# The norms of two graph layers: sums of squares and the last scaling on ScalarE, in pieces one row apart

## The reference

```python
h_self = x @ W1[i] + b1[i]
h_nb = x @ W0[i] + b0[i]
agg = segment_sum(h_nb[edge_src], edge_dst, num_segments=n)
x = concatenate([h_self, agg], axis=-1) @ W2[i] + b2[i]
x = x / std(x, axis=-1, ddof=1, keepdims=True)
```

## Time and profile before

| | us |
|---|---|
| median of 3 runs | 2557.65 |
| lowest, highest | 2557.43, 2562.71 |
| the profiled execution's own time | 2560.65 |
| its span | 2558.9 |

### The profile page before, as it was taken

One profiled execution on the slowest core, in us unless ns is written; L12 is line 12 of the kernel. 1 busy time (PEld: TensorE's weight loads), 2 busy tenths in 40 slices (PEclk: granted clock), 3 DMA queues, 4 the chain that ended last, 5 costly groups with the idle time before them and its releaser, 6 DMA issues. The chain is left out here.

```text
span 2558.9 us, 59508 instructions
## 1 busy us (share of the span) xinstructions
PE 2064.3 (81%) x23672; PEld 1900.6 (74%) x23672; DVE 1740.2 (68%) x4728; ACT 885.0 (35%) x1180; POOL 1249.9 (49%) x1021
## 2 busy tenths in 40 slices
PE   4494569999999999997883897888887578888870
PEld 4232269999999999997883896777776567777760
DVE  8999975555555555565655995776676456777656
ACT  0395510000000000001211563777674066777620
POOL 0200047777777777760000452666664346666651
PEclk9995579999999999998996898999999689999975
DMA  3593012232323232320003882334433034434321
GB/s 130 170 408 130 1 19 25 21 30 21 30 21 30 21 30 21 30 21 14 1 1 125 301 319 68 114 120 129 133 114 115 19 92 129 125 114 133 122 78 28
DMA packets 150635, 227.44 MB, mean 89 GB/s; under 512 B 87617, under 2 KB 109793, under 8 KB 147074
## 3 DMA queue, kind: packets, MB, share of 16 engines
q1 hardware_dynamic: 70418, 186.31, 20.1%
q0 software_dynamic: 74688, 28.51, 11.5%
q10 hardware_dynamic: 5296, 9.47, 1.2%
HBM read 123.37 MB, written 100.84 MB: 88 GB/s over the span
## 5 line engine op out<-in xcount | busy, mean ns | idle before, releaser
L637 PE MATMUL ps<-parts,at 128*128 128x192 f16 x11250 | 947.9, 248 | 23.6 <-POOL at L669 13.7
L637 PEld LDWEIGHTS ps<-parts,at 128*128 128x128 f16 x11250 | 940.1, 99 | 25.9 <-issue 24.2
L1706 PE MATMUL ps<-yparts,source_onehots_c 128*128 128x192 f16 x7000 | 679.3, 250 | 123.6 <-issue 110.4
L1706 PEld LDWEIGHTS ps<-yparts,source_onehots_c 128*128 128x128 f16 x7000 | 579.1, 99 | 188.7 <-issue 172.0
L679 POOL DMA_INDIRECT weight_matrix<-w,place x392 | 609.6, 1555 | 175.0 <-issue 93.8
L1498 POOL DMA_INDIRECT messages_c<-y_table,srci_sb x504 | 498.2, 988 | 380.2 <-PE ps L1706 157.4
L767 DVE SCALAR_TENSOR_TENSOR t<-ps,coef,g 128x96 f32<-128x96 f32 x400 | 127.1, 318 | 246.4 <-PE ps L637 200.6
L1581 DVE TENSOR_SCALAR source_onehots_c<-sources_spread,shift 128x1280 f16<-128x1280 f16 x512 | 282.1, 561 | 0.4
L707 ACT ACTIVATE ea_limbs<-ea_in,ea_scale 128x392 f16<-128x392 f32 x32 | 19.9, 622 | 743.6 <-DMA ea_in<-in_eaT 735.4
L1526 ACT ACTIVATE source_gaps_c<-sources_spread,unshift 128x1280 f16<-128x1280 f16 x188 | 256.4, 1364 | 23.3 <-DVE source_onehots_c L1581 5.1
L1630 DVE SCALAR_TENSOR_TENSOR messages_c<-messages_c,brk 128x96 f32<-128x96 f32 x784 | 249.6, 318 | 17.4 <-issue 0.2
(11 more groups left out here) (374 smaller groups left out, 1858.5 us busy)
## 6 DMA issues: line engine op xcount, KB each, us to landing
weight_matrix<-blank SPq DMA_DIRECT2D x27, 1600.0 KB
weights<-weight_matrix SPq DMA_DIRECT2D x25, 1728.0 KB
run_max<-messages_c SPq DMA_DIRECT2D x28, 960.0 KB
ea_c<-edge_limbs SPq DMA_DIRECT2D x28, 896.0 KB
edge_limbs<-ea_limbs SPq DMA_DIRECT2D x128, 98.0 KB
run_max<-messages_c SPq DMA_DIRECT2D x28, 384.0 KB
sources_spread<-sources_by_tile ACTq DMA_DIRECT2D x26, 320.0 KB
messages_c<-y_table,srci_sb POOLq DMA_INDIRECT x504
```

Source lines behind the costliest of these rows:

```text
L637: mm = nc.tensor.matmul(m.ps[:, bank, 0:2 * D], m.at[:, s, blk * P:(blk + 1) * P], parts[:, s, :], start=(s == 0), stop=(s == NB - 1))
L1706: return nc.tensor.matmul(m.ps[:, i // 2, at:at + 2 * D], hot[:, b, i * P:(i + 1) * P], parts[:, b, :], start=(b == 0 and i % 2 == 0), sto ...
```

## The change

For groups 0 to 3 of both layers (`beside`), the norm is cut into pieces that stand one row step apart. VectorE sums the rows and writes the negative mean (`negative_mean`). ScalarE then runs five ACTIVATEs with the function Square, one per block of 128x96, with the negative mean as a bias pointer and the sum over the row as accumulator output (`sum_squares`). One step on VectorE turns the sums into variances (`spread_of`) and ScalarE takes the root. One more step on VectorE refines the root and scales `y` (`unit_spread`); in the second layer the scaling and the residual are one instruction per block, with the root as a pointer, followed by the layer norm's negative mean. The layer norm goes the same way, two rows later: squares by ScalarE four rows behind, variance and root five behind, refinement and a shift (minus mean times inverse root) on VectorE six behind, and then ScalarE writes `x` by five ACTIVATEs with the function Identity, scale and bias as pointers. The last group of each layer keeps the old pieces at their old places. `norms` numbers the norms for the semaphores, `closing(i, lag)` names the group whose last row stands `lag` rows back. TensorE's program is unchanged.

```diff
@@ -861,7 +861,12 @@
         mx, amx, scales = sem("y_max"), sem("y_max_all"), sem("scale_known")
         highs, ready = sem("y_high_parts"), sem("y_parts")
         b = c.enter_context(nc.Block())
+        meaned, squared, shifts = sem("group_means"), sem("squares_summed"), sem("norm_shifts")
+        xs = sem("x_scaled")
         last_of = lambda q: q % ENDS == ENDS - 1
+        closing = lambda i, lag: (i - lag) // ENDS if 0 <= i - lag < NB and last_of(i - lag) else None
+        beside = lambda g: g is not None and g < NEND - 1
+        norms = lambda layer, g: (NEND - 1) * layer + (g if layer == 0 else 2 * g)
         ends = lambda g: slice(g * ENDS, (g + 1) * ENDS)
 
         @b.sync
@@ -883,6 +888,14 @@
 
         @b.scalar
         def _(a):
+            def sum_squares(n, g):
+
+                a.wait_ge(meaned, n + 1)
+                for j, q in enumerate(range(g * ENDS, (g + 1) * ENDS)):
+                    summed = nc.scalar.activation(deep[:, j, :], y[:, q, :], ACT.Square, bias=m.st1[:, q:q + 1],
+                                                  accum_out=m.st2[:, q:q + 1])
+                summed.then_inc(squared, 1)
+
             for layer in range(2):
                 back = 1.0 / XSCALE if layer == 0 else un[:]
                 roots = ROOTS_SAGE + layer * NEND
@@ -910,12 +923,30 @@
                             a.wait_ge(outd, n - 2)
                         nc.scalar.activation(aggT[:, (n - 1) % 2, :], m.ps[0:D, 4 + (n - 1) % 2, 0:P],
                                              ACT.Copy).then_inc(aggtc, 1)
-                    if 2 <= i <= NB + 1 and last_of(i - 2):
-                        g = (i - 2) // ENDS
+                    g = closing(i, 2)
+                    if beside(g):
+                        sum_squares(norms(layer, g), g)
+                    elif g is not None:
                         square_root(nc, a, m, roots + (g if layer == 0 else 2 * g) + 1, m.st2[:], ends(g))
-                    if layer == 1 and 3 <= i <= NB + 2 and last_of(i - 3):
-                        g = (i - 3) // ENDS
+                    g = closing(i, 3)
+                    if beside(g):
+                        square_root(nc, a, m, roots + (g if layer == 0 else 2 * g) + 1, m.st2[:], ends(g))
+                    elif g is not None and layer == 1:
                         square_root(nc, a, m, roots + 2 * g + 2, m.st2[:], ends(g))
+                    if layer == 1:
+                        g = closing(i, 4)
+                        if beside(g):
+                            sum_squares(norms(layer, g) + 1, g)
+                        g = closing(i, 5)
+                        if beside(g):
+                            square_root(nc, a, m, roots + 2 * g + 2, m.st2[:], ends(g))
+                        g = closing(i, 6)
+                        if beside(g):
+                            a.wait_ge(shifts, g + 1)
+                            for q in range(g * ENDS, (g + 1) * ENDS):
+                                moved = nc.scalar.activation(m.x[:, q, :], y[:, q, :], ACT.Identity, bias=m.st1[:, q:q + 1],
+                                                             scale=m.st2[:, q:q + 1])
+                            moved.then_inc(xs, 1)
                 if layer == 0:
                     a.wait_ge(scales, 1)
                     for g in range(NEND):
@@ -953,6 +984,33 @@
                 do(nc.vector.tensor_reduce(m.st2[:, blk], deep[:], AX.X, ALU.add))
                 nc.vector.scalar_tensor_tensor(m.st2[:, blk], m.st2[:, blk], 1.0 / (D - 1), m.padcol[:, blk], ALU.mult,
                                                ALU.add).then_inc(m.var_ready, 1)
+
+            def negative_mean(g):
+
+                blk = ends(g)
+                do(nc.vector.tensor_reduce(m.st1[:, blk], y[:, blk, :], AX.X, ALU.add))
+                nc.vector.tensor_scalar(m.st1[:, blk], m.st1[:, blk], -1.0 / D, None, ALU.mult).then_inc(meaned, 1)
+
+            def spread_of(n, g):
+
+                v.wait_ge(squared, n + 1)
+                nc.vector.scalar_tensor_tensor(m.st2[:, ends(g)], m.st2[:, ends(g)], 1.0 / (D - 1), m.padcol[:, ends(g)],
+                                               ALU.mult, ALU.add).then_inc(m.var_ready, 1)
+
+            def unit_spread(layer, g, n):
+
+                inverse_root(nc, v, do, m, n, m.st2[:], ends(g))
+                if layer == 0:
+                    do(nc.vector.tensor_tensor(y[:, ends(g), :], y[:, ends(g), :], bc_last(m.st2[:, ends(g)], D), ALU.mult))
+                    v.sem_inc(normed, 1)
+                    do(nc.vector.tensor_reduce(gmx[:, g:g + 1], y[:, ends(g), :].rearrange("p i f -> p (i f)"), AX.X,
+                                               ALU.max, apply_absolute_value=True))
+                else:
+                    for q in range(g * ENDS, (g + 1) * ENDS):
+                        last = nc.vector.scalar_tensor_tensor(y[:, q, :], y[:, q, :], m.st2[:, q:q + 1], m.x[:, q, :],
+                                                              ALU.mult, ALU.add)
+                    do(last)
+                    negative_mean(g)
 
             spread_biases()
             for layer in range(2):
@@ -966,8 +1024,10 @@
                                                        agg[:, n % 2, :], ALU.mult, ALU.add).then_inc(aggc, 1)
                     if n == 1:
                         fold_weights()
-                    if 3 <= i <= NB + 2 and last_of(i - 3):
-                        g = (i - 3) // ENDS
+                    g = closing(i, 3)
+                    if beside(g):
+                        spread_of(norms(layer, g), g)
+                    elif g is not None:
                         blk = ends(g)
                         inverse_root(nc, v, do, m, roots + (g if layer == 0 else 2 * g) + 1, m.st2[:], blk)
                         do(nc.vector.tensor_tensor(y[:, blk, :], y[:, blk, :], bc_last(m.st2[:, blk], D), ALU.mult))
@@ -980,8 +1040,21 @@
                             centre(nc, do, m, y, deep[:], blk)
                             nc.vector.tensor_scalar(m.st2[:, blk], m.st2[:, blk], 1.0 / D, EPS, ALU.mult,
                                                     ALU.add).then_inc(m.var_ready, 1)
-                    if layer == 1 and 4 <= i and last_of(i - 4):
-                        g = (i - 4) // ENDS
+                    g = closing(i, 4)
+                    if beside(g):
+                        unit_spread(layer, g, roots + (g if layer == 0 else 2 * g) + 1)
+                    g = closing(i, 5)
+                    if layer == 1 and beside(g):
+                        v.wait_ge(squared, norms(1, g) + 2)
+                        nc.vector.tensor_scalar(m.st2[:, ends(g)], m.st2[:, ends(g)], 1.0 / D, EPS, ALU.mult,
+                                                ALU.add).then_inc(m.var_ready, 1)
+                    g = closing(i, 6)
+                    if layer == 1 and beside(g):
+                        inverse_root(nc, v, do, m, roots + 2 * g + 2, m.st2[:], ends(g))
+                        nc.vector.tensor_tensor(m.st1[:, ends(g)], m.st1[:, ends(g)], m.st2[:, ends(g)],
+                                                ALU.mult).then_inc(shifts, 1)
+                    g = closing(i, 4)
+                    if layer == 1 and g == NEND - 1:
                         blk = ends(g)
                         inverse_root(nc, v, do, m, roots + 2 * g + 2, m.st2[:], blk)
                         do(nc.vector.tensor_tensor(m.x[:, blk, :], y[:, blk, :], bc_last(m.st2[:, blk], D), ALU.mult))
@@ -997,7 +1070,10 @@
                                                 ALU.add).then_inc(outc, 1)
                         if last_of(i - 2):
                             v.wait_ge(outc, q + 1)
-                            deviation((i - 2) // ENDS)
+                            if beside((i - 2) // ENDS):
+                                negative_mean((i - 2) // ENDS)
+                            else:
+                                deviation((i - 2) // ENDS)
                 if layer == 0:
                     nc.vector.tensor_reduce(gm[:], gmx[:], AX.X, ALU.max).then_inc(mx, 1)
                     v.wait_ge(amx, 1)
```

## The result

| | before | changed |
|---|---|---|
| median of 5 runs, us | 2558.33 | 2542.80 |
| lowest, highest | 2557.43, 2568.17 | 2542.21, 2547.56 |
| ratio, 95% interval | | 0.9943 (0.9930 to 0.9955) |
| profiled execution, own time | 2560.65 | 2547.56 |
| its span | 2558.9 | 2545.8 |

A forecast was written before the change was run, and what follows sets the result against it. TensorE was taken to wait in the second graph layer on VectorE's block and ScalarE's queue. Gains of 15.3 us there and 1.1 in the first layer, 16.4, took the median of 2557.65 to 2541.3; range 2536 to 2551.

The forecast's parts named there:

- 23.6 us lost in the second layer: Second layer's stretch before the change: 86.04 us against 62.4 undisturbed, lost to TensorE's waits and its lower clock.
- VectorE's unbroken block: Second layer before: VectorE's 5.6 us block and ScalarE's place in the queue behind it are the whole stall.
- c = 0.35: On ScalarE, time in us from one square with summed output to the next: 0.22, 0.08 for the read, 0.05 for less overlap.
- estimate of 0.27 from the Trainium skill: Alternative time in us between ScalarE's squares, before any accumulator read; the four-row wait would then be under 0.9.
- Four rows behind: Second layer's layer norm squares: ScalarE starts 4.0 us after T, the row's turn on TensorE; TensorE waits 1.3, 0.8 in group three.
- Two rows behind: Second layer: scaled copies six rows behind delay the following group's squares; waits of 0.6, 0.6 and 1.0 us, sum 2.2.
- The last row 2.8: Second layer, fourth group: the squares' wait falls on the last row, where no product hides it; 2.8 us more.
- No clock loss: Second layer: no new wait inside it is over 1.3 us, so no loss from TensorE's lower clock is counted.
- One rival's "every wait over about 2.5 costs the lower clock": Rival that ScalarE becomes the bound: slower past about 0.65 us per square, 2567 us at 0.8; chance 0.04.
- Second layer 15.3, first 1.1: Gains in us: second layer 23.6 lost before less 8.3 of new waits; first layer 1.1 of 1.8 lost.
- The last group's chain and the scaled copies are covered: Layer tails cost what they did; the fourth group's copies, at most 1.8 us, run beside the last group's deviation on VectorE.
- The rival of a serial accumulator: ScalarE's accumulator read is serial, 0.5 to 0.6 us per square; gain only 3 to 9 us, about 2551.5; chance 0.17.

The follow-up runs named there:

- spread_on_vector: The kernel before, second layer only: layer norm's mean, squares, variance four rows behind instead of three, last scaling five instead of four, all on VectorE; ratio 0.9949.
- squares_twice: The changed kernel with each summed square done twice on ScalarE, the first time into memory that nothing reads; ratio 1.0016 to before.
- x_on_vector: The changed kernel with x of groups 0 to 3 written by five VectorE operations instead of ScalarE's scaled copies; ratio 0.9929 to before.
- copies_first: The changed kernel with layer norm's squares behind the next row's copies, five rows behind, and that norm's later pieces one row later; ratio 0.9949 to before.
- changed_again: The changed kernel itself, run again on the chip of the later runs; 2352.6 us against 2367.8 for the kernel before, ratio 0.9932.

## Why the prediction was right

Point by point, by its own steps.

- *23.6 us lost in the second layer.* By the lengths of its steps, before, some 17 of them were waits and 6 the clock. The stretch fell to 71.39 with clock 1.00. spread_on_vector comes to 71.86 by order alone, which bears out the argument of VectorE's unbroken block and of ScalarE's queue behind it. The 6 us a group taken off VectorE, which the prediction names first among the parts of the change, were not needed for it: moving them without removing them gives 14.2 of the 14.7 us.
- *c = 0.35.* Measured 0.36: an ACTIVATE of 0.36 and a read of 0.19 that begins before its end (1305.31, 1305.59, 1305.68). The line of the squares, all 60 of them:

```profile
L895 ACT ACTIVATE spread_sq<-y_sb,st x60: 357/359/376, 1217.8 to 1352.9; 128x96 f32<-128x96 f32 x60
L895 ACT ACTIVATION_READ_ACCUMULATOR spread_sq<-y_sb,st x60: 185/187/188, 1218.1 to 1353.1; 128x1 f32 x60
```

  The value of c was right by luck in its parts, two errors that cancel: from a square's start to its read's start are 0.27 rather than the 0.22 of the pair in the earlier trace rows, which both read PSUM, and the read adds 0.09 rather than 0.13. No run has squares without the read, so this split is read off the rows. The prediction's estimate of 0.27 from the Trainium skill (ScalarE: Activation LUTs, What ACT_TABLE_LOAD costs), for an ACTIVATE with a pointer in a row and without the read, agrees with the 0.27 to 0.28 that the trace shows from a square's start to its read's start.
- *Four rows behind: ScalarE starts at T+4.0, wait 5c - 0.49 = 1.3.* Started at T+3.99, steps longer by 1.34, 1.21 and 0.77 (forecast 1.3, 1.3, 0.8). In squares_twice the first group's wait is 3.33, by the formula 3.1.
- *Two rows behind 0.6, 0.6, 1.0.* 0.63, 0.63 and 1.05; x_on_vector, where only 0.3 of the last is left, shows that ScalarE's scaled copies make them.
- *The last row 2.8.* Its step is 3.86, where an undisturbed one is 0.92: 2.9.
- *No clock loss.* The granted clock is 1.00 over the stretch. One rival's "every wait over about 2.5 costs the lower clock" does not hold, though: in squares_twice a wait of 2.25 cost it and one of 2.83 did not.
- *Second layer 15.3, first 1.1.* 14.65 and 1.38. The sum, 16.4, against 16.0 in these stretches. Of the 0.65 missing in the second layer, 0.4 is the step after each wait, 0.07 longer than undisturbed (2.66 instead of 2.59), six times, which I had not counted; the rest is 0.1 in the sum of the waits two rows behind and 0.1 at the last row.
- *The last group's chain and the scaled copies are covered.* From the last turned aggregate to the end of x 13.6 us against 13.4; the fourth group's copies ran from 1355.76 to 1357.66, ten us before the end of x.

The rival of a serial accumulator, at 0.17, falls by the rows: the read overlaps both neighbours. The Trainium skill (same page, Rules for kernel authors) puts adds and multiplies on VectorE for its rate per element, which it gives for bf16. The tiles here are fp32: the five scalings take 1.90 us on ScalarE and 1.29 on VectorE (x_on_vector), and having them on ScalarE costs 1.8 us of stretch, through the waits two rows behind that the prediction had in its sum at 2.2. How much of that is the longer 1.90 and how much the place in the queue is not separated by a run.

## What to carry to other kernels

When three engines pass a row round, measure the time between the turns of the bottleneck engine in an undisturbed row, and give each side piece a deadline from it: when must the next row's hand-over be done, and what stands in front of it on each of the two queues, the wait at a queue's head included. A piece that moves to the neighbouring row step can bring nearly as much as one that moves to another engine (14.2 of 14.7 us of the stretch here, 12.8 of 14.5 counted to the end of x), and one that moves to an idle engine can still cost time where it stands ahead of that engine's own hand-over. Collect the pieces of all groups per step before moving one: in copies_first a piece freed one step and jammed another, and the same waiting in longer lumps cost the clock besides.

## What the runs showed of the hardware that I had not expected

- ScalarE's accumulator read (ACTIVATION_READ_ACCUMULATOR, 128x1) is 187 ns long, more than twice VectorE's 83, but starts 0.09 before the ACTIVATE's end and lets the next one start 0.10 before its own; a summed output costs 0.09 us per ACTIVATE in a row.
- Waits of 1.2 to 1.3 us inside the layers left TensorE's clock at the upper level each time. Longer ones went both ways, and not in the order of their length: behind the three waits of copies_first (2.45, 2.40, 2.40) the next step was 4.30, 2.65 and 4.41, and in squares_twice the product behind a wait of 2.25 took 3.39 instead of 2.23 while the one behind 2.83 took 2.23.
- The same kernel had a span of 2545.8 us in the result and of 2350.8 in changed_again. The first product of the edge convolutions comes at nearly the same time in both (1542.3 and 1543.1), and behind it lie 1003 us in the first and 808 in the second. In the edge convolutions of the first, TensorE stood idle 103.5 us ahead of the products L1782 for "issue" (no wait that the profile shows); in the second it stood idle 6.5 us ahead of them for any reason. What makes that idle time, and whether it is the chip, no run here shows.
